# An attention and feed-forward kernel: reordering the hand-over to its last stage

## The reference

```
x = x + xattn(layernorm(x), ctx)      # 16 heads of 32; q, k, v and the softmax rounded to 8-bit steps
x = x + ffn(layernorm(x))

ffn(x):   xq    = round(x * 127/max|x|) / scale           # per token
          x1,x3 = split(xq @ w13.T)                       # 512 -> 2 x 1408
          gated = relu(x1)**2 * x3
          inner = rmsnorm(gated) * norm_w
          iq    = round(inner * 127/max|inner|) / scale   # per token
          out   = iq @ w2.T                               # 1408 -> 512
```

## Time and profile before

| what | value |
|---|---|
| median of 3 runs | 1853.44 us (1852.49 to 1860.74) |
| the profiled execution's own time | 1846.16 us |
| its span | 1844.4 us |
| busy: DVE, PE, POOL, ACT | 1690.0, 1630.5, 1430.2, 1390.8 us |
| granted TensorE clock, mean | 0.982 of full |

### The profile page before, as it was taken

The page is one execution under the profiler, slowest core; times in us unless marked ns, Lnnn a source line. Parts: engine busy times, 40 slices in busy tenths (PEclk is TensorE's granted clock), DMA queues, the critical chain, the costliest instruction groups (busy, mean ns, idle before and its releaser), DMA issues.

```text
span 1844.4 us, 42223 instructions
## 1 busy us (share of the span) xinstructions
PE 1630.5 (88%) x17032; PEld 1152.6 (62%) x17032; DVE 1690.0 (92%) x2670; ACT 1390.8 (75%) x1362; POOL 1430.2 (78%) x1159
## 2 busy tenths in 40 slices
PE   7997899988888889888888898888889888789998
PEld 6884666666565666655566666555555555478876
DVE  6869999999999999999999999999999999877664
ACT  2447889888888988889889988897888888733221
POOL 1433889999889899989899999998999898752222
PEclk9999999999999999999999999999999999889999
DMA  5578998999899988898999899789888998832221
GB/s 179 198 222 202 198 192 177 179 199 175 168 181 203 188 182 185 171 182 175 189 202 177 173 202 176 148 168 187 173 170 160 208 182 150 175 107 49 63 58 47
DMA packets 851535, 310.00 MB, mean 168 GB/s; under 512 B 784967, under 2 KB 813965, under 8 KB 851213
## 3 DMA queue, kind: packets, MB, share of 16 engines
q1 hardware_dynamic: 851340, 307.29, 81.4%
HBM read 74.26 MB, written 39.59 MB: 62 GB/s over the span
## 4 chain that ended last, share of the span: by engine, by line
DVE 58%; PE 20%; POOL 8%; issue 7%; DMA 4%; ACT 1%; SPq 1%; POOLq 0%; DVEq 0%; ACTq 0%
DVE S L1280 53%; POOL PT L1502 6%; PE PS L868 5%; PE PK L905 3%; PE PS L703 2%; DMA PP<-Pr 2%; PE PS L735 2%; PE PK L674 2%; PE PK L676 2%; DVE MJ L1306 1%; PE PO L676 1%; DVE kam L1171 1%; PE PO L674 1%; DVE VMX L1175 1%; ACT Pr L1075 1%
## 5 line engine op out<-in xcount | busy, mean ns | idle before, releaser
L1280 DVE TENSOR_SCALAR_CACHE_REDUCE S<-PS,SQN 128x1536 f32<-128x1536 f32 (+1 forms) x768 | 1282.9, 1714 | 18.4 <-PE PS L735 9.1
L1502 POOL CAST PT<-PP 128x1536 uint16<-128x1536 uint8 (+1 forms) x800 | 1100.1, 1420 | 112.5 <-DMA PP<-Pr 111.2
L1075 ACT ACTIVATE Pr<-S,MS 128x5888 uint8<-128x5888 f32 x200 | 1041.7, 5209 | 170.3 <-DVE MJ L1306 121.0
L735 PE MATMUL PS<-KT,QT 96*128 96x512 bf16 (+1 forms) x2496 | 631.9, 372 | 154.1 <-DVE S L1280 141.7
L754 PEld LDWEIGHTS PO<-VI,PT 128*128 128x128 f16 x9200 | 338.2, 96 | 197.3 <-POOL PT L1502 30.5
L735 PEld LDWEIGHTS PS<-KT,QT 96*128 96x128 bf16 (+1 forms) x2496 | 190.6, 98 | 365.8 <-DVE S L1280 133.0
L754 PE MATMUL PO<-VI,PT 128*128 128x32 bf16 x9200 | 356.1, 178 | 18.2 <-ACT AO L1029 10.1
L676 PE MATMUL PK<-CT,WG 128*128 128x128 f32 (+1 forms) x1288 | 211.7, 292 | 6.8 <-DMA CT<-ctxt 6.8
L674 PE MATMUL PK<-WG,CT 128*128 128x128 f32 (+1 forms) x1288 | 210.7, 293 | 5.7 <-ACT VV L941 3.7
L676 PEld LDWEIGHTS PK<-CT,WG 128*128 128x128 f32 x1288 | 168.0, 193 | 9.7 <-issue 7.6
L674 PEld LDWEIGHTS PK<-WG,CT 128*128 128x128 f32 (+1 forms) x1288 | 167.1, 192 | 8.1 <-issue 6.3
(11 more groups left out here) (156 smaller groups left out, 1554.3 us busy)
## 6 DMA issues: line engine op xcount, KB each, us to landing
CT<-ctxt SPq DMA_DIRECT2D x180, 256.0 KB, 3.1
k_rows<-KS SPq DMA_DIRECT2D x39, 512.0 KB, 4.1
q_rows<-QS SPq DMA_DIRECT2D x13, 512.0 KB, 4.6
W13F<-w13T SPq DMA_DIRECT2D x12, 352.0 KB, 3.5
PP<-Pr SPq DMA_TRANSPOSE x200, 5.8
XT<-x SPq DMA_DIRECT2D x12, 256.0 KB, 4.3
XR<-x SPq DMA_DIRECT2D x12, 256.0 KB, 3.3
base_rows<-XO SPq DMA_DIRECT2D x12, 256.0 KB, 3.4
```

The costliest lines, as they stand in the source:

```text
L735: last = pe.matmul(PS[n % 2][p0:p0 + r, f:f + w], QT[h % 3][0:PARTS * HD, q0:q0 + r], KT[h % 3][0:PARTS * HD, c * CHUNK + f:c * CHUNK + f ...
L1075: act.activation(Pr[i % 2].rearrange("p t q b -> p t b q"), S[i % 2].rearrange("p (t b q) -> p t b q", b=2, q=P), ACT.Exp, bias=MS[:, i % ...
L1280: v.tensor_scalar(S[i % 2][:, c * CHUNK:c * CHUNK + CW[c]], PS[n % 2][:, 0:CW[c]], neg_step, None, ALU.mult, ALU.min, accum_out=MN[:, i % ...
L1502: gp.tensor_copy(PT[i % 2][:, 2 * t0:2 * t1, :].rearrange("p (t b) q -> p t b q", b=2), PP[i % 2][:, t0:t1, :].bitcast(U8).rearrange("p t ...
```

## The change

The parts of the diff, in words:

- **Load behind the transposition.** SP issues the load of block 3 of w13 after the transposition of step 198.
- **Halves.** ACT makes the high part of block 3, and DVE its low part, in two halves of 1408 columns. The first half is what `expand(0, 0)` reads, the second what `expand(0, 1)` reads; `expand(0, 1)` now waits for its own. ACT puts `root(1)` between its two halves, DVE `quantise_tokens(1)` between its two. All later counts of `f_hi` and `f_lo` grow by one.
- **Tile 1 and tile 2 earlier.** DVE runs `add_residual(1)` straight behind `quantise_tokens(0)`, `token_stats(1)` behind the widening of tile 0, and `add_residual(2)`, `token_stats(2)`, `quantise_tokens(2)` ahead of the loop, so ahead of the first split of w2 and of `hidden(0)`. PE runs `front_turn(2)` and `project(2)` ahead of `expand(0, 0)`; ACT its copy `transposed(2)` behind `values_out` of step 197, and `root(2)` after the first relu and square. SP turns tile 2 ahead of the transposition of IQ of tile 0; POOL widens tile 2 ahead of its rounding of tile 0.
- **Spare products.** PE makes 22, 16 and 8 products of a tile of ones with 256 columns into PS[0], whose contents nothing reads, around `front_turn(2)` and `project(2)`.

The core of the diff:

```diff
+BUSY = (22, 16, 8)
...
                 sp.wait_ge(M["s_exp"], i + 1)
-                if i == NA - 2:
-                    k = NK - 1
-                    sp.dma_start(halves(k)[2], w13T[k * P:(k + 1) * P, :]).then_inc(M["f_w1"], 16)
...
                 sp.dma_start_transpose(PP[i % 2], ...).then_inc(s_tr[i % 2], 16)
+                if i == NA - 2:
+                    k = NK - 1
+                    sp.dma_start(halves(k)[2], w13T[k * P:(k + 1) * P, :]).then_inc(M["f_w1"], 16)
...
             for s in range(1, NT + 3):
-                if s < NT:
+                if s < NT and s != 2:
                     turn_tokens(s)
                 if s == 1:
...
                     load_w2(2)
+                    turn_tokens(2)
...
                 if t:
                     pe.wait_ge(M["f_g" if half else "f_rl"], t)
+                elif half:
+                    pe.wait_ge(M["f_lo"], NK + 1)
...
+            def busy(n):
+                for _ in range(n):
+                    pe.matmul(PS[0][:, 0:2 * P], ones[:, :], ones[:, :].unsqueeze(1).to_broadcast([P, 2, P]),
+                              start=True, stop=True)
+
             last_values(NA - 3)
             pe.wait_ge(M["s_ev"], NC_ * NA)
+            busy(BUSY[0])
+            front_turn(2)
+            busy(BUSY[1])
+            project(2)
+            busy(BUSY[2])
             expand(0, 0)
             last_values(NA - 2)
-            front_turn(2)
             expand(0, 1)
             last_values(NA - 1)
             for s in range(2, NT + 3):
-                if s < NT:
+                if 2 < s < NT:
                     project(s)
...
+            values_out(NA - 3)
+            transposed(2)
             act.wait_ge(M["f_w1"], 16 * (WSP + 1))
             act.wait_ge(M["f_hi"], NK - 1)
-            act.activation(halves(NK - 1)[0], halves(NK - 1)[2], ACT.Copy).then_inc(M["f_hi"], 1)
-            values_out(NA - 3)
+            last_high(0)
             root(1)
+            last_high(1)
             for s in range(1, NT + 1):
-                if 1 < s < NT:
+                if 2 < s < NT:
                     root(s)
...
                 if s == 1:
                     values_out(NA - 2)
-                if s + 1 < NT:
+                    root(2)
+                if 2 < s + 1 < NT:
                     transposed(s + 1)
...
-                if t + 2 < NT:
+                if 2 < t + 2 < NT:
                     add_residual(t + 2)
...
             quantise_tokens(0)
+            add_residual(1)
             low_part(2)
             v.wait_ge(M["f_xit"], 16)
             v.tensor_scalar(XIF[0], XIT, 1.0, None, ALU.mult).then_inc(M["f_xif"], 1)
-            low_part(3)
+            token_stats(1)
+            low_part(3, 0)
+            quantise_tokens(1)
+            low_part(3, 1)
             v.wait_ge(M["s_exp"], NA)
             v.reciprocal(...)
-            add_residual(1)
+            add_residual(2)
+            token_stats(2)
+            quantise_tokens(2)
             for s in range(1, NT + 3):
-                if s < NT:
+                if 2 < s < NT:
                     token_stats(s)
                     quantise_tokens(s)
...
             widen_tokens(1)
             normalise(H // 2 - 1)
+            widen_tokens(2)
             for s in range(1, NT + 2):
                 if s == 2:
                     split_w2(2)
-                if 1 < s < NT:
+                if 2 < s < NT:
                     widen_tokens(s)
```

More of the change, by code:

```diff
@@ L897, in _ @@
                     if t == 0:
-                        pe.wait_ge(M["f_lo"], NK + len(W2_SPLIT))
+                        pe.wait_ge(M["f_lo"], NK + 1 + len(W2_SPLIT))
                     if s < NT:
@@ L1096, in split_w2, with last_high @@
                 act.wait_ge(s_w2[n], 16)
-                act.wait_ge(M["f_hi"], NK + n)
+                act.wait_ge(M["f_hi"], NK + 1 + n)
                 act.activation(W2[:, lo:hi, 0, :], W2F[:, lo:hi], ACT.Copy).then_inc(M["f_hi"], 1)
+            def last_high(half):
+                cols = slice(half * FF, (half + 1) * FF)
+                act.activation(halves(NK - 1)[0][:, cols], halves(NK - 1)[2][:, cols], ACT.Copy).then_inc(M["f_hi"], 1)
+            values_out(NA - 3)
+            transposed(2)
             act.wait_ge(M["f_w1"], 16 * (WSP + 1))
             act.wait_ge(M["f_hi"], NK - 1)
-            act.activation(halves(NK - 1)[0], halves(NK - 1)[2], ACT.Copy).then_inc(M["f_hi"], 1)
-            values_out(NA - 3)
+            last_high(0)
             root(1)
+            last_high(1)
             for s in range(1, NT + 1):
-                if 1 < s < NT:
+                if 2 < s < NT:
                     root(s)
@@ L1307, in _, with low_part @@
                                 accum_out=MS[:, i % 2, 0:1]).then_inc(M["s_mx"], 1)
[L1309 to L1313, removed]
+            def low_part(k, half=None):
+                cols = slice(0, 2 * FF) if half is None else slice(half * FF, (half + 1) * FF)
+                high, low, full = [part[:, cols] for part in halves(k)]
+                v.wait_ge(M["f_hi"], k + 1 + (half == 1))
+                v.wait_ge(M["f_lo"], k + (half == 1))
                 v.tensor_tensor(low, full, high.bitcast(F32), ALU.subtract).then_inc(M["f_lo"], 1)
@@ L1318, in split_w2 @@
                 lo, hi = W2_SPLIT[n]
-                v.wait_ge(M["f_hi"], NK + n + 1)
-                v.wait_ge(M["f_lo"], NK)
+                v.wait_ge(M["f_hi"], NK + n + 2)
+                v.wait_ge(M["f_lo"], NK + 1)
                 v.tensor_tensor(W2[:, lo:hi, 1, :], W2F[:, lo:hi], W2[:, lo:hi, 0, :].bitcast(F32),
@@ L1534, in split_w2 @@
                 lo, hi = W2_SPLIT[n]
-                gp.wait_ge(M["f_hi"], NK + n + 1)
-                gp.wait_ge(M["f_lo"], NK)
+                gp.wait_ge(M["f_hi"], NK + n + 2)
+                gp.wait_ge(M["f_lo"], NK + 1)
                 gp.tensor_tensor(W2[:, lo:hi, 1, :], W2F[:, lo:hi], W2[:, lo:hi, 0, :].bitcast(F32),
```

## The result

| | before | after |
|---|---|---|
| median of 12 runs | 1852.58 us | 1855.62 us |
| ratio, 95% interval | | 1.0027 [1.0014, 1.0040] |
| profiled execution: span | 1844.4 us | 1853.7 us |
| end of the last exponential | 1605.23 | 1613.88 |
| from there to the end of the span | 239.17 | 239.82 |

Two later comparisons of the same two kernels gave 1.0008 [0.9993, 1.0023] and 1.0026 [1.0003, 1.0048]. So the change costs 0.1 to 0.3% by the three ratios, of which one can't be told from 1, and all lie within the 0.5% that one measurement tells from nothing. The forecast was a saving of 5.4 us and a median of 1848.0; the measured 1855.62 lies 1.1 us above the upper end of the range.

A forecast was written before the change was run, and what follows sets the result against it. DVE paces attention, left unchanged; behind it two breaks in PE's products (8.56 and 5.20 us idle) bind. Tile 0's second product 5.9 us earlier, less 0.5 for reordered queues: 1853.44 - 5.4 = 1848.0 us; range 1842 to 1854.5.

The forecast's parts named there:

- The load behind the transposition: SP's queue: step 198's transposition lands at 1601.4, some 5.5 us earlier; XIF(0) at 1611.3, 1.2 us later.
- Spare products hide, and the clock is full: PE ahead of `expand(0, 0)`: at most 0.4 us sticks out; the product runs 1611.3 to 1616.5, 1.8 us earlier.
- rival C: Clock falls again in the some 3 us wait ahead of `expand(0, 1)`; 2.5 us saved, 1851; chance 0.15.
- the second break: PE idle 5.20 us ahead of `expand(2, 0)`, then slow clock, 7.1 us in all; forecast gone, with tile 2's XIF by 1634.
- Halves and tile 1: DVE after XIF(0): first half about 1614.3, XI(1) 1618.8, second half 1620.7; G(0) at 1628.5, 2.3 us later.
- X1(3) ... comes in `hidden(1)`, ... some 6.4 later: DVE: `hidden(1)` starts at 1638.1, X1(3) some 6.4 later at 1644.5, when tile 0's second product starts.
- 14.1 us from G(0): Tile 0's IQ, transposed and widened, is ready for its second product at 1628.5 + 14.1 = 1642.6, in time.
- 5.9 us earlier: Tile 0's second product starts at 1644.5 instead of 1650.46; the steady part starts 5.9 us earlier.
- B: Rival: the load does not hold XI(0)'s transposition, so the front gains too; about 9.5 us saved, 1844; chance 0.20.
- D: Rival: DVE's queue ahead of the gate binds; G(0) behind 1636, at 1638 the kernel 2 us slower, 1855.5; chance 0.08.
- The steady part shifts by a constant: Tiles from 3 on: all shifted by one constant, the steady part starting 5.9 us earlier, 5.4 after 0.5 off.

The follow-up runs named there:

- e4: Changed kernel with the load of w13's last block ahead of the transposition again, as in the kernel before; ratio to before 1.0006 [0.9993, 1.0018].
- e7: Changed kernel with ACT's second and third high part and POOL's last low part of w2 moved earlier; ratio to before 0.9988 [0.9971, 1.0006].
- e15: Changed kernel run again unchanged, its third profile, on the chip of the two shifted kernels; ratio to before 1.0026 [1.0003, 1.0048].
- e2: Changed kernel run again unchanged, for a second profile; ratio to before 1.0008 [0.9993, 1.0023].
- e8: Changed kernel with both low-part halves together ahead of tile 1's quantisation and the w2 splits early; ratio to before 1.0003 [0.9987, 1.0018].
- e13: Changed kernel with 22 more spare products in attention steps 147 and 149; ratio to before 1.0011 [0.9994, 1.0027].
- e14: Changed kernel with 44 more spare products in attention steps 147 and 149; ratio to before 0.9998 [0.9980, 1.0017].

## Why the prediction was wrong, point by point

- **The load behind the transposition.** Right in time (cast of step 198 at 1601.7 on before's scale, forecast 1601.4; XIF(0) at 5.5, forecast 6.1), and right that it loses 1 us on XIF(0). e4: worth nothing.
- **Spare products hide, and the clock is full.** Right for the first half product, 5.4 us against the forecast 5.2. I booked 1.8 us for it. It was lost in the wait of 3.5 us that I had myself worked out as "some 3 us" and made rival C with a chance of 0.15. C was what happened, in all three profiles of the changed kernel: 8.0, 7.9, 6.8. The evidence was in rows 3: idle for 2 us, and the clock fell. C was priced too well, though: 2.5 us were still to be saved, because the second break was taken as won.
- **Halves and tile 1.** The second half product at 15.6 (forecast 1620.7 - 1605.2 = 15.5): right. G(0) at 25.5 against the forecast 23.3: off by 2.2, where the clock cost 2.6.
- **The second break.** XIF(2) in time and no idle ahead of tile 2's half product: right. The step that failed is "X1(3) ... comes in `hidden(1)`, ... some 6.4 later". It took 1658.64 - 1649.55 = 9.1 us from G(1), as GW collided with POOL's split of w2 and then with the widening. In the kernel before POOL's split ran at 1636, beside tile 2's quantisation; the change took that quantisation from there, and the same 3.5 us met GW instead. e7 took GW of tile 1 out of the collision, and 2.2 us came back; its other gains e15 had too. The product then waits for IQF, which is a second term that was too small: 14.1 us from G(0) were forecast, 17.2 (e7) and 18.1 (after) measured. One part of it stands above: POOL's GW of tile 0, 3.41 us, started 0.19 us behind DVE's split of w2 (2.28), and took 1.44 for tile 1. So without the collision on X1 the second product still could not have started at the forecast 1644.5.
- **5.9 us earlier** was thus 0.3: the second product was forecast 39.3 us behind the end of attention and started at 44.9, of which 2.2 us are G(0)'s and 3.4 the stretch from G(0) to it (16.0 forecast, 19.4 measured). B and D did not happen: DVE's queue ahead of the gate was no bound while the clock was low, and G(0) at 25.5 is well ahead of D's 30.8.
- **The range** ended at 1854.5, 1 us above the median before, for a spread given as 1846 to 1853, though the three runs on record went to 1860.74; and that nothing is won at all had no chance of its own. It is what came.
- **The steady part shifts by a constant.** Wrong, and not asked: the tiles have no slack (XIF(4) was ready 0.05 us ahead of its product, 1677.94 and 1677.99 before), and which tile is late depends on where instruction fetches fall.
- **What stays open.** The marks explain 2 us lost up to G(2) in two of three profiles of the changed kernel and 1 us won in the third; behind G(2) the three took 182.8, 189.0 and 182.7, the kernel before 183.5 and 183.6. Of this, 1.6 us hang on the clock of the kernel's very last product alone: 6.8 to 6.9 us in both profiles of before and in e2, 5.3 in after and e15. The last stage as a whole is 241.0 us in the mean of three against 238.7 of two, which fits 0.1 to 0.3% but, at this scatter, doesn't prove its parts.

The Trainium skill (SBUF — State Buffer, "Who interferes with whom") has the port pair as a lock that the later instruction waits for, for the whole of the earlier. The row of 4.85 us agrees: it begins 0.14 behind POOL's 3.51 and ends 1.48 behind its end, 1.63 being its length alone in e7. I had the rule in hand and applied it to the casts, and not to the POOL instruction that the change set against GW.

## What to carry to other kernels

A wait worked out in a sum must be priced twice: its length, and the clock of what stands behind it. When work is taken out of the way of a long instruction on the other engine of a shared port, ask what that instruction meets instead; e8 shows that moving it once more can only change its victim. Spare products kept the clock here where they ended 0.5 and 1.3 us ahead of the product that needed it, not where they ended 4.4 us ahead, and in no case was a gain of the whole kernel shown for them; and where every tile of a pipeline has no slack, a few microseconds won ahead of it are within what late transfers give and take.

## What the runs showed that I had not expected

An engine's instruction fetch (one packet of queue q8, 0.02 MB, or of q14, 0.01 MB) in flight with the transposition of XI delays it. In the kernel before one such tile, at 1772.85, met a fetch and landed in 4.0 us, against the median; in the steady part of all 17 profiles (tiles 3 to 12) none of the 136 transpositions without a fetch took more than 3.6, the 16 that met q8 took 3.7 to 5.6, and the 18 with q14 alone 3.1 to 4.2. Where q8 meets them is a matter of how many instructions PE has issued, so an edit anywhere ahead of the last stage, even 22 products in attention, moves it. With 5.2 us (e2) it was the start of a loss of 6.3 us against the first profile, and only the start: 0.6 is the later landing, 1.5 the widening that by it met a GW on DVE, 2.7 the clock of the half product (8.14 instead of 5.41), and 1.6 the clock of the kernel's last product, which has nothing to do with it.

Attention, the same instructions in all kernels but for e13 and e14, ended between 1605.2 and 1617.9 in seventeen profiles. Against that scatter the last stage's 1 to 5 us are read only from marks counted from its own start.
